# Causal attention on one Trainium2 core: where the future scores of the transposed tiles are removed

## The reference, cut to what matters

```python
scores = jnp.einsum('bqhd,bkhd->bhqk', q, k)
scores = scores + jnp.einsum('bqr,bkr->bqk', q_rope, k_rope)[:, None]
scores = scores / scale
causal = jnp.triu(jnp.ones((Tt, Tt), dtype=bool), k=1)
scores = jnp.where(causal[None, None], -jnp.inf, scores)
w = jax.nn.softmax(scores, axis=-1)
attn = jnp.einsum('bhqk,bkhd->bqhd', w, v).reshape(Bb, Tt, D_MODEL)
return attn @ W_o
```

## Time and profile before

| what | value |
|---|---|
| runs shown | 2260.83 us median (2260.19 to 2264.94) |
| the profiled execution, its own time | 2264.79 us |
| its span, first to last instruction | 2263.0 us |
| PE busy | 1820.8 us (80%) |
| DVE busy | 1432.0 us (63%) |
| ACT busy | 1164.7 us (51%) |
| POOL busy | 454.7 us (20%) |
| mean granted TensorE clock | 0.874 of full |

### The profile page before, as it was taken

The page is one execution under the profiler, slowest core; times in us unless marked ns, Lnnn a source line. Parts: engine busy times, 40 slices in busy tenths (PEclk is TensorE's granted clock), DMA queues, the critical chain, the costliest instruction groups (busy, mean ns, idle before and its releaser), DMA issues. The chain is left out here.

```text
span 2263.0 us, 42539 instructions
## 1 busy us (share of the span) xinstructions
PE 1820.8 (80%) x15621; PEld 971.6 (43%) x15621; DVE 1432.0 (63%) x2872; ACT 1164.7 (51%) x2304; POOL 454.7 (20%) x602
## 2 busy tenths in 40 slices
PE   4669999999999841998353999999999996439982
PEld 1236666666665531776230222222222222327761
DVE  4556666666666159542057999999999993585410
ACT  2306666666666410333150888888888885103330
POOL 0000000000000100688730000000000000016886
PEclk9859999999999955799675999999999998557996
DMA  3474471744440010343331000000000000113333
GB/s 104 146 137 83 74 130 24 129 85 71 86 87 2 1 40 21 85 69 60 31 130 61 16 16 25 22 16 29 17 16 30 16 2 1 40 28 87 66 59 63
DMA packets 97485, 124.79 MB, mean 55 GB/s; under 512 B 14696, under 2 KB 57584, under 8 KB 97264
## 3 DMA queue, kind: packets, MB, share of 16 engines
q1 hardware_dynamic: 72336, 104.59, 19.7%
q0 software_dynamic: 24960, 17.68, 6.0%
HBM read 87.17 MB, written 35.95 MB: 54 GB/s over the span
## 5 line engine op out<-in xcount | busy, mean ns | idle before, releaser
L940 DVE TENSOR_REDUCE mx<-wide 128x2 f32<-128x1024 f32 x512 | 603.7, 1220 | 45.9 <-PE wide L868 33.7
L968 ACT ACTIVATE pT<-bank 128x512 f32<-128x512 f32 x1024 | 555.3, 595 | 85.6 <-PE bank L861 78.4
L700 ACT ACTIVATE pT<-bank 128x512 f32<-128x512 f32 (+3 forms) x768 | 358.4, 490 | 286.8 <-PE bank L567 268.7
L868 PE MATMUL wide<-k_st,q_st 48*128 48x512 bf16 x1024 | 351.5, 398 | 37.1 <-DMA k_st<-qk_parts 24.1
L861 PE MATMUL bank<-q_st,k_st 51*128 51x512 bf16 x1024 | 355.0, 387 | 21.9 <-ACT pT L968 5.3
L669 DVE TENSOR_REDUCE mx<-wide 128x1 f32<-128x640 f32 (+3 forms) x256 | 258.9, 1022 | 136.2 <-PE wide L578 133.5
L877 PE MATMUL bank<-pT,vst 128*32 128x256 f32 x4096 | 328.3, 392 | 0.1
L567 PE MATMUL bank<-q_st,k_st 122*128 122x512 f32 (+3 forms) x768 | 316.0, 414 | 3.8 <-ACT pT L700 1.8
L578 PE MATMUL wide<-k_st,q_st 120*128 120x512 f32 (+3 forms) x768 | 314.3, 416 | 4.8 <-DMA k_st<-rope_split 3.4
L861 PEld LDWEIGHTS bank<-q_st,k_st 51*128 51x128 bf16 x1024 | 91.4, 93 | 316.2 <-ACT pT L968 274.0
L1438 POOL DMA_INDIRECT acc_rows<-yg,idxs x128 | 200.4, 1566 | 52.0 <-issue 36.3
(11 more groups left out here) (225 smaller groups left out, 1965.0 us busy)
## 6 DMA issues: line engine op xcount, KB each, us to landing
q_st<-rope_split SPq DMA_DIRECT2D x72, 256.0 KB
k_st<-rope_split SPq DMA_DIRECT2D x72, 256.0 KB
qk_split<-parts SPq DMA_DIRECT2D x8, 1024.0 KB, 4.1
q_st<-qk_split SPq DMA_DIRECT2D x96, 64.0 KB
k_st<-qk_split SPq DMA_DIRECT2D x96, 64.0 KB
qk_parts<-parts SPq DMA_DIRECT2D x8, 768.0 KB, 3.4
xn_rows<-xn SPq DMA_DIRECT2D x8, 512.0 KB, 3.2
w1b<-in_L_ffn_w SPq DMA_DIRECT2D x16, 256.0 KB, 2.9
```

What stands on the lines that cost most here:

```text
L700: e.activation(pT[:, u % NPB, q0:HALF], bank[u % 2][:, q0:HALF], ACT.Exp, scale=scale).then_inc(s_p, 1)
L868: e.matmul(wide[w % 2][:, r * HALF:(r + 1) * HALF], q_st[at][64 * r:64 * r + MROW, pair, q0:q0 + P], k_st[at][64 * r:64 * r + MROW, pair, ...
L940: e.tensor_reduce(mx[G % 2][:, kh, pair:GH:2, c], wide[w % 2][:, :].rearrange("p (r k) -> p r k", r=2), AX.X, ALU.max).then_inc(s_sf, 1)
L968: e.activation(pT[:, u % NPB, :], bank[u % 2][:, :], ACT.Exp, scale=scale).then_inc(s_p, 1)
```

## The change

The mask matmul of the transposed scores is gone. A score in a diagonal tile starts its bank by itself. ACT takes the exponential of the future positions too. When the four exponentials of a diagonal quad are done, one `affine_select` on POOL writes zero over the future positions of the four tiles in `pT`, 128 partitions by 4 times 128 elements. `weigh` waits for this select as well (`s_cut`). In POOL's stream the wait for `s_m` and the DMA of the maxima move from the t of the split to a later t, two after PE's transposition of the maxima is due.

```diff
+            def at_diagonal(quad):
+
+                s, J, kc, j, q0 = unit(quad * GH)
+                return kc >= J * CPH
+
+            def cuts_to(quad):
+
+                return sum(at_diagonal(n) for n in range(quad + 1))
+
                     def t_score(u):
                         s, J, kc, j, q0 = unit(u)
-                        at, diag = s % NBUF, kc >= J * CPH
-                        if diag:
-                            e.matmul(bank[u % 2][:, q0:q0 + P], identb[:, :], mask_kq[:, :], start=True, stop=False,
-                                     skip_group_check=True)
+                        at = s % NBUF
                         e.matmul(bank[u % 2][:, q0:HALF], k_st[at][0:KROW, j, kc * P:(kc + 1) * P],
-                                 q_st[at][0:KROW, J, j, q0:HALF], start=not diag, stop=True,
-                                 skip_group_check=True).then_inc(s_st, 1)
+                                 q_st[at][0:KROW, J, j, q0:HALF], start=True, stop=True).then_inc(s_st, 1)
...
                             e.wait_ge(s_p, PRIME + (quad + 1) * GH)
+                            e.wait_ge(s_cut, PRIME + cuts_to(quad))
                             weigh(quad, 0)
                             weigh(quad, 1)
...
                             e.tensor_tensor(mx2[G % 2][:, 1, :], mx[G % 2][:, :], mx2[G % 2][:, 0, :], ALU.subtract).then_inc(s_m2, 1)
+                        w = t + LEAD - 2 if t + LEAD - 2 < LAST else t + LEAD - 4
+                        if w in turns and (w < LAST) == (t + LEAD - 2 < LAST):
+                            G = turns[w][0]
                             e.wait_ge(s_m, PRIME + G + 1)
                             dst = q_st[G // 2 % NBUF][KS:KROW, G % 2, :, :].bitcast(F32)
                             e.dma_start(dst.rearrange("i j x -> i (j x)"), nmp[G % 2][:, :].bitcast(F32)).then_inc(s_row[G % 2], 16)
+                        if t % 2 == 0 and 2 <= t <= LAST and at_diagonal(t // 2 - 1):
+                            quad = t // 2 - 1
+                            q0 = unit(quad * GH)[4]
+                            e.wait_ge(s_p, PRIME + (quad + 1) * GH)
+                            tiles = pT[:, quad * GH % NPB:quad * GH % NPB + GH, q0:q0 + P]
+                            e.affine_select(out=tiles, in_=tiles, compare_op=ALU.is_ge, fill=0.0, base=0,
+                                            pattern=[[0, GH], [1, P]], channel_multiplier=-1).then_inc(s_cut, 1)
                         if t - 4 in ends:
                             H = ends[t - 4]
                             if H % 2 and H // 2 + 2 < STEPS:
```

More of the change, by code:

```diff
@@ L500, in attend_causal @@
             s_oev, s_ot, s_y, s_ych = sem("o_ev"), sem("o_turned"), sem("y"), sem("y_chain")
-            s_vz, s_vs = sem("v_init"), sem("v_stage")
+            s_vz, s_vs, s_cut = sem("v_init"), sem("v_stage"), sem("future_cut")
             buf, give_back = of_phase()
```

## The result

The changed kernel takes 2324.14 us (median of 4, 2321.52 to 2327.76), the kernel before 2260.51 us beside it. The ratio is **1.028**, with an interval of 1.026 to 1.030: 63.6 us slower. The forecast had the sign and less than half of the size, 2287.6 us. The measured time lies 6 us above its range.

What follows compares the result with a forecast made beforehand. PE's queue was taken to bound the kernel. Masks gain 15 x 1.38 = 20.7 us, stalls lose 15 x 3.17 = 47.5, so +26.8 us: 2287.6 us on the median, range 2258 to 2318.

Steps and rivals of the forecast that it cites:

- the hidden-select rival: POOL is in time at t = 4 and t = 20, every select hides: 2229 us, chance 0.13.
- 3.17 + 0.72: Per step: both stalls delay the weighs by 3.17 us; masks of the two 256-column quads, 0.36 each, are swallowed.
- 2.80 us of slack: Second half's 384-column quad: time from its exponentials' end to its weigh, to cover a 0.65 us select and two hand-overs.
- the first rival: POOL in time at t = 4 and t = 20, all selects hidden, change faster: 2229 us, chance 0.13.
- Where it is not hidden: Part on t = 4 and t = 20: select queues behind POOL's wait, cast and subtraction; PE stalls, 47.5 us lost.
- It comes 1.61 later: Second half, weigh at the end of t = 21: moves from 2.10 to 3.71 us after t = 20 starts.
- so 1.56 later: First half, weigh at the end of t = 5: moves from 2.14 to 3.70 us after t = 4 starts.
- I take both as zero: Last step: masks worth about 0.5 us together, and the very last select's exposed 0.65 plus hand-over, both counted as nothing.
- a granted clock below 0.99 in the body: Listed sign that the forecast is wrong, for the body of the causal attention; no size given.
- the slow select: Rival: POOL's select takes 1.66 us, so the 30 stalls cost 30.3 us more: 2318 us, chance 0.09.
- The cancellation: Rival: each mask worth 0.12 us, 43.2 gained, against 40.3 lost with a 0.41 select: 2258 us, chance 0.08.

Runs made afterwards that it cites:

- both runs with the clock held: The changed kernel with fill matmuls in PE's waits at t = 21 and t = 5: 15 and 10 (ratio 1.011), or 7 and 10 (1.0114).
- the half fill: The changed kernel with 7 fill matmuls in PE's wait at t = 21 and 10 at t = 5: 2284.7 us, ratio 1.0114 to the kernel before.

## Why the prediction was right and wrong

**Right.** PE's queue bounds the stage, and the select is hidden in six of eight quads: the waits of PE for POOL are the 30 forecast and the one at the very end. A hidden select costs nothing: the runs with the selects first and without any are 0.4 us apart. The stalls are where they were forecast, 30 of them, behind the cast in POOL's queue, within 0.05 us of the forecast distance from the start of t. The select takes 0.63 for 0.65. The Trainium skill (GPSIMD Engine Reference, section 3.1) gives 0.77 by its tight loop and, as an estimate from its 12 cycles per element, about 5 by its branching code; the measurement lies below both. The moved DMA and the second wait cost nothing. Removing the masks with the selects in time gives a ratio of 0.9859, where the hidden-select rival said 2229 us, a ratio of 0.986.

**A little off.** The masks of a step are worth 38.1 - 36.1 = 2.0 us, with 2.1 forecast. Those of the first half's narrowest quad gave 0.11 (351.51 to 354.05 in the run with the selects first, 2.54 us, against 2.65 before) instead of 0.25. The two stalls with the clock held cost 39.6 - 36.1 = 3.5 us per step, where the forecast's terms had 3.17 + 0.72 = 3.9. These partly cancel, and the sum stands where it was put, 1.011 in both runs with the clock held, 1.012 forecast; that it is so near is in part luck. The 2.80 us of slack, too, were read at a quad whose select is not hidden: the weigh at 277.85 is the very one that stalls in the changed kernel. And of the two distances set against the first rival, 0.98 runs to the end of the subtraction and 0.42 only to the start of the cast; to the end of the subtraction it is 0.90 in the first half (252.85 + 0.21, less 252.16). Neither changes the sum.

**The step that failed** is the one under "Where it is not hidden": "It comes 1.61 later", "so 1.56 later", times 15, is 47.5 us. This prices a stall as the time by which the weigh is late. It takes the work behind the stall at the speed it had before. In the changed kernel PE stood idle for 1.8 us, the clock fell to its lower level behind half of the stalls or more (15 of 30 in the first profile, 20 of 30 in the second), and the work of the next microseconds ran at half speed, in some steps for 10 us. The term that is missing is 42.1 - 39.6 = 2.5 us per step, 36.5 us over the 14.5 steps between the first and the last cast (616.8 less the 580.3 of the half fill), and 41.0 us by the two kernels on one chip.

The last step, of which the forecast said "I take both as zero", adds to it. From the last cast to the start of the last weigh the traces show 34.3 us before, 45.0 and 39.5 in the two profiles of the changed kernel, and 38.7 in the half fill. About 1.7 of each difference is the last of the 30 stalls, which the forecast had (the weigh starts 1.2 behind its cast instead of 0.5 ahead of it). That leaves 9.0, 3.5 and 2.7 us, with 27.3, 10.2 and 3.4 us of half clock in the stretch. So the clock went unpriced there too, and what the last select costs alone stays open.

The text named "a granted clock below 0.99 in the body" as a sign of error but gave it no price, no rival and no place in the range. In the body of the kernel before no wait of PE shows in the list of waits, and its matmuls have 2.0 us of idle time in 561 us (174 to 735), so no row of that stage could bound it. A bound was to be had from the size of the work behind a stall. The 128-column quad behind t = 21 takes 2.6 us at full clock (278.64 to 281.27 in the timeline of before); run once at half, it would cost 2.6 more, and 30 of them 78 us, an estimate. The upper end of the range should have reached for that.

Of the rivals, the slow select (2318 us) is nearest in time and false in its mechanism. The cancellation fell with the measured masks. The hidden select is not what this kernel does, but it is what it does when POOL's order is changed.

## What to carry to other kernels

Before a wait is put on a second engine, look at what that engine is itself waiting for in its queue at that moment: being idle for over nine tenths of the stage was no help to POOL behind one wait for DVE, and moving the select ahead of that wait turned 2.8% slower into 1.4% faster. On PE a new stall can have two prices, its own length and the clock behind it: here 3.5 us per step for the first and 2.5 for the second. Where a wait can't be avoided, shorten the idle stretch: 7 and 10 small matmuls in the two waits of a step kept the clock here.

## What the runs showed of the hardware that was not expected

An idle time of 1.8 us between long stretches of full work was enough for the granted clock to fall from 1.00 to 0.50, but not each time: behind 15 of 30 such stalls in one execution of the changed kernel and 20 of 30 in another. It came back after 3.4 us in the step shown, and after 10.2 in every third step (in one of them the clock is 0.50 in all of 240 to 250 us). Idle times of 0.94 and 0.65 us, in the same places, did nothing. Which of a step's two equal stalls is followed by half clock differed between kernels (after t = 5 in all 15 steps once t = 21 was filled) and between two executions of the same kernel, so the program alone does not settle it; what does stays open. The Trainium skill (TensorE: Matmul & The Clock Gate, Part 1) has the two levels and the activity that decides between them, and the rows shown agree: the clock is 1.00 or 0.50 in a stretch of steady state, and between them only where a stretch holds a change.
